# Lane marks by 32 narrow instructions, number products on GpSimd, and the inversion ahead of the turn sums

## The reference

```python
x  = L0_attn_u                                # (4, 512, 128)
xn = _layernorm(x)
# branch 1: a state-space layer, 4 heads of 64, state 128
z, xh, Bg, Cg, dd_dt, dd_A, trap, angles = split(xn @ W_in)
theta = cumsum(angles * dt)                   # over a sequence
K = rope(rmsnorm(Bg) * B_norm_w + B_bias, theta)
Q = rope(rmsnorm(Cg) * C_norm_w + C_bias, theta)
y = (chunked scan of decayed Q K^T products over xh) + D * xh
attn = (y * silu(z)) @ W_out
# branch 2: 16 experts, the best 2 of each token
probs = softmax(xn @ Wr + br); vals, idx = top_k(probs, 2)
for e in range(16):
    h = silu(xn @ W1[e]) * (xn @ W3[e])
    out += combine[:, e] * layernorm(h @ W2[e], gamma[e], beta[e])
return x + attn + out
```

## Time and profile before

| What | us |
|---|---|
| median of 3 runs | 285.36 (285.24 to 285.71) |
| the profiled execution | 283.92 |
| its span on the core | 282.2 |
| TensorE busy (matmul) | 252.1 |
| VectorE busy | 221.4 |
| GpSimd busy | 208.3 |
| ScalarE busy | 150.0 |

### The profile page before, as it was taken

One profiled execution on the slowest core, in us unless ns is written; L12 is line 12 of the kernel. 1 busy time (PEld: TensorE's weight loads), 2 busy tenths in 40 slices (PEclk: granted clock), 3 DMA queues, 4 the chain that ended last, 5 costly groups with the idle time before them and its releaser, 6 DMA issues.

```text
span 282.2 us, 7396 instructions
## 1 busy us (share of the span) xinstructions
PE 252.1 (89%) x2157; PEld 217.9 (77%) x2161; DVE 221.4 (78%) x604; ACT 150.0 (53%) x512; POOL 208.3 (74%) x284
## 2 busy tenths in 40 slices
PE   2999997799999999999999999999999999999600
PEld 0857964787897998899889979997998899889500
DVE  4778998778787969796979688787969796978446
ACT  1766996593456453755364645456453745363033
POOL 8656997698887787888887878887787875665400
PEclk9999999799999999999999999999999999999965
DMA  5630888665779778977889687988878987870096
GB/s 155 224 94 7 273 261 286 173 187 164 208 228 281 253 224 250 275 234 221 250 288 237 232 249 202 303 245 270 262 225 242 274 245 231 255 220 30 21 264 182
DMA packets 68856, 61.55 MB, mean 218 GB/s; under 512 B 6609, under 2 KB 52305, under 8 KB 68817
## 3 DMA queue, kind: packets, MB, share of 16 engines
q1 hardware_dynamic: 66256, 55.83, 65.5%
q0 software_dynamic: 2560, 5.25, 6.5%
HBM read 56.27 MB, written 4.78 MB: 216 GB/s over the span
## 4 chain that ended last, share of the span: by engine, by line
PE 60%; DVE 17%; ACT 6%; issue 6%; DMA 4%; POOL 4%; SPq 1%; DVEq 1%; POOLq 0%; ACTq 0%
PE bank L874 16%; PE bank L917 6%; PE bank L817 5%; PE bank L809 4%; PE bank L869 4%; PE bank L801 3%; PE bank L763 2%; PE bank L851 2%; PE bank L768 2%; DMA decay<-res_dram 2%; PE bank L913 2%; DVE rot L1360 2%; DVE sd L1376 2%; PE bank L833 2%; PE bank L860 1%
## 5 line engine op out<-in xcount | busy, mean ns | idle before, releaser
L874 PE MATMUL bank<-blkT,w_up 128*128 128x128 f32 x512 | 64.7, 280 | 1.5 <-DVE xrow L1410 0.6
L874 PEld LDWEIGHTS bank<-blkT,w_up 128*128 128x128 f32 x512 | 61.4, 195 | 4.2 <-issue 2.3
L633 POOL DMA_INDIRECT res_dram<-xrow,sidx x40 | 40.7, 1017 | 21.9 <-DVE xrow L1438 17.7
L580 POOL DMA_INDIRECT blk<-xn_dram,gidx x40 | 42.7, 1067 | 8.5 <-issue 7.3
L917 PE MATMUL bank<-w,xrow 128*128 128x128 f32 x256 | 34.6, 278 | 0.3 <-DVE xrow L1425 0.3
L1113 ACT ACTIVATE xrow<-bank 128x512 f32<-128x512 f32 x40 | 25.2, 629 | 15.2 <-PE bank L874 11.2
L917 PEld LDWEIGHTS bank<-w,xrow 128*128 128x128 f32 x256 | 31.1, 192 | 1.6 <-issue 1.6
L1410 DVE TENSOR_TENSOR xrow<-xrow,bank 128x512 f32<-128x512 f32 x40 | 27.3, 682 | 4.4 <-issue 4.2
L1342 DVE SCALAR_TENSOR_TENSOR kq<-sd,rms,bias_kq 128x512 f32<-128x512 f32 x32 | 23.2, 765 | 8.5 <-POOL rms L591 7.5
L626 POOL TENSOR_TENSOR rstd<-mv,mhalf 128x1 f32<-128x1 f32 x40 | 25.2, 629 | 0.3
L1107 ACT ACTIVATE blkT<-bank 128x128 f32<-128x128 f32 x40 | 12.2, 306 | 24.5 <-PE bank L860 20.9
(11 more groups left out here) (250 smaller groups left out, 617.1 us busy)
## 6 DMA issues: line engine op xcount, KB each, us to landing
w_up<-in_L_ffn_W_dram SPq DMA_DIRECT2D x96, 256.0 KB
w<-in_L_ffn_W_dram SPq DMA_DIRECT2D x48, 256.0 KB
e_row<-e_dram SPq DMA_DIRECT2D x16, 256.0 KB
decay<-l_dram SPq DMA_DIRECT2D x4, 512.0 KB, 6.0
gam<-in_L_ffn_gamma_dram SPq DMA_DIRECT2D x32, 64.0 KB
shift_y<-in_L_ffn_beta_dram SPq DMA_DIRECT2D x32, 64.0 KB
acc<-in_L_attn_u_dram SPq DMA_DIRECT2D x4, 256.0 KB, 3.7
xn_dram<-xrow SPq DMA_DIRECT2D x4, 256.0 KB, 5.1
```

The lines of the kernel that those rows point to most:

```text
L580: g.indirect_dma_start(out=blk[:, b % SLOTS, :], out_offset=None, in_=xn_dram, in_offset=bass.IndirectOffsetOnAxis(ap=gidx[:, entry(b):ent ...
L633: g.indirect_dma_start(out=res_dram, in_=res[:, b % HALF, :], in_offset=None, out_offset=bass.IndirectOffsetOnAxis(ap=sidx[:, entry(b):ent ...
L874: last = m(bank[out][:, c * P:(c + 1) * P], w_up[:, u % SETS, n, c * P:(c + 1) * P], blkT[:, b % 2, :], start=True, stop=True)
```

## The change

- Lane marks: two instructions of 2048 columns (`tensor_tensor`, both operands broadcast) become 32 of 128 columns (`tensor_scalar`, the token's lane number as a column operand in fp32).
- Block marks: the two compares stand one behind the other ahead of the lane marks; the products with the numbers become `mark(k)` on GpSimd, between the cuts.
- The expert of each block is worked out on GpSimd, ahead of the angle products; `pick_experts` goes from VectorE.
- The products and reductions that give the slots are done for both choices at once.
- TensorE does `invert(0)` and `invert(1)` in front of `sum_turns(1)` to `sum_turns(3)`; three dummy matmuls (`WARM_BLOCKS`) go.
- On VectorE `cut_turns(0)` and `mean_square(0)` come ahead of the row indices; `cut_turns(2)` and `cut_turns(3)` move back in `begin()`; in tile 1 `norm_kq` comes behind `product`.
- On GpSimd two of the eight cuts come behind the first gather, the first norm's power ahead of the second gather, and `weigh_q(0)` into tile 1.
- On ScalarE the logarithm of the gains comes ahead of the compares, the first squares two tiles earlier, the table load and the first sines earlier in `begin()`; tile 1 has another order.
- Some semaphores are merged, some scratch tiles share or change places.

```diff
-        bn_kq = sd[:, 0:2, :]
+        bn_kq = sd[:, 2:4, :]
...
+            pool.wait_ge(counted, 1)
+            g.tensor_scalar(behind[0:NU], full_n[0:NU], NE - 0.5, -2.0 * NE, ALU.is_gt, ALU.mult)
+            link(g.tensor_tensor(full_n[0:NU], full_n[0:NU], mix_n[0:NU], ALU.add))
+            link(g.tensor_tensor(full_n[0:NU], full_n[0:NU], behind[0:NU], ALU.add))
+            g.tensor_scalar(full_n[0:NU], full_n[0:NU], 2.0 * NE, 2.0 * (NE - 1), ALU.add, ALU.min)\
+                .then_inc(expert_ready, 1)
...
-            for t in range(SUMMED, NT):
-                cut_rows(t)
+            def mark(k):
+
+                pool.wait_ge(spots_ready, k + 1)
+                rows = row_h[:, k * NT:(k + 1) * NT, :]
+                g.tensor_tensor(rows, rows, bc(val_h[:, k * NT:(k + 1) * NT], NB, 1), ALU.mult).then_inc(marks_ready, 1)
+            cut_rows(SUMMED)
+            mark(0)
+            cut_rows(SUMMED + 1)
+            mark(1)
+            cut_rows(SUMMED + 2)
+            cut_rows(SUMMED + 3)
+            cut_rows(NT - 4)
+            cut_rows(NT - 3)
             pool.wait_ge(xn_out, 16 * NBATCH)
             pool.wait_ge(gidx_ready, 1)
+            gather(0)
+            cut_rows(NT - 2)
+            cut_rows(NT - 1)
...
-            gather(0)
+            rms_pow(0)
             gather(1)
-            rms_pow(0)
...
                 if first and t > 0:
                     rms_pow(t)
+                if t == 1:
+                    weigh_q(0)
...
-                if first:
+                if first and t > 0:
                     weigh_q(t)
...
                 pe.wait_ge(hot_ready, k + 1)
+                pe.wait_ge(marks_ready, k + 1)
...
             invert(0)
+            invert(1)
             sum_turns(1)
             sum_turns(2)
-            invert(1)
             sum_turns(3)
...
-                for _ in range(WARM_BLOCKS):
-                    m(bank[6][:, :], ones_h[:, :], neg_h[:, :, :].rearrange("p h i -> p (h i)"), start=True, stop=True)
...
+            act.wait_ge(g_ready, 1)
+            a(lnG, gmax, ACT.Ln).then_inc(lng_ready, 1)
...
-            act.wait_ge(g_ready, 1)
-            a(lnG, gmax, ACT.Ln).then_inc(lng_ready, 1)
...
-                if t == SUMMED + 4:
+                if t == SUMMED + 2:
                     squares(0)
...
-                out_block(0)
                 nc.scalar.preload_act_table_set("silu_and_others")
                 act.wait_ge(rest_in, 16 * RESTS)
+                out_block(0)
+                sines(0)
                 silu(0)
                 out_block(1)
-                sines(0)
                 silu(1)
...
-                if first:
+                if t == 1:
+                    squares(t)
+                    sines(t)
+                    out_block(b0 + 1)
+                    silu(b0)
+                elif first:
                     sines(t)
                     squares(t)
+                if first:
                     weigh(t)
                     gates(t)
                     move_x(t)
...
-            pick_experts()
             dve.wait_ge(pos_used, 1)
-            tt(pick, oh1, posb, ALU.mult)
-            link(tt(sc1, oh2, posb, ALU.mult))
-            v.tensor_reduce(slot[:, 0, :], pick, X, ALU.add)
-            link(v.tensor_reduce(slot[:, 1, :], sc1, X, ALU.add))
+            link(tt(pick, chosen, bc(posb, TOPK, 0), ALU.mult))
+            link(v.tensor_reduce(slot, pick, X, ALU.add))
...
-            one_hots(0)
-            one_hots(1)
+            for k in range(TOPK):
+                tt(row_h[:, k * NT:(k + 1) * NT, :], bc(iota_k, NT, 0), bc(blk_h[:, k, :], NB, 1), ALU.is_equal)                    .then_inc(spots_ready, 1)
                 if k == 0:
                     dve.wait_ge(expert_psum, 1)
+                    ts(blk_e[:, :], bank[3][0:1, 0:NU], 0.5, None, ALU.mult).then_inc(blk_e_ready, 1)
+            for k in range(TOPK):
+                for t in range(NT):
+                    last = ts(lane_h[k][:, t, :], iota_l, s_lane[:, k, t:t + 1], None, ALU.is_equal)
+                last.then_inc(hot_ready, 1)
+            cut_turns(0)
+            mean_square(0)
...
-                mean_square(0)
-                for b in range(NBATCH - 1):
-                    cut_turns(b)
+                cut_turns(1)
                 dve.wait_ge(rest_in, 16 * RESTS)
 
-                dve.wait_ge(theta_psum, NBATCH)
+                dve.wait_ge(theta_psum, 1)
                 weigh_bc(0)
                 norm_kq(0)
+                cut_turns(2)
                 product(0)
-                cut_turns(NBATCH - 1)
                 rot_cosine(0)
                 rotate(0)
+                cut_turns(3)
                 product(1)
...
-                    norm_kq(t)
+                    if t > 1:
+                        norm_kq(t)
...
                     product(b0)
+                if t == 1:
+                    norm_kq(t)
```

More of the change, by code:

```diff
@@ L211, in build @@
         turns = scratch([P, NT, NH * NA])
-        lg, rt, sc1, posb, pick = (scratch([P, NT, NE]) for _ in range(5))
+        rt, posb = (scratch([P, NT, NE]) for _ in range(2))
+        pick = scratch([P, TOPK, NT, NE])
+        lg, sc1 = pick[:, 0], pick[:, 1]
         lnG = scratch([P, NT, NH])
@@ L232, in build @@
         e2 = scratch([P, NT])
-        oh1 = scratch([P, NT, NE])
-        oh2 = scratch([P, NT, NE])
+        chosen = scratch([P, TOPK, NT, NE])
+        oh1, oh2 = chosen[:, 0], chosen[:, 1]
         halves = scratch([P, NE])
@@ L1008, in _ @@
             act.wait_ge(act_step, 1)
-            a(sp_e, sp_x, ACT.Exp, scale=-1.0).then_inc(spe_ready, 1)
+            a(sp_e, sp_x, ACT.Exp, scale=-1.0).then_inc(spx_ready, 1)
             act.wait_ge(spu_ready, 1)
-            a(sp_l, sp_u, ACT.Ln).then_inc(spl_ready, 1)
-            act.wait_ge(spl_ready, 1)
-            a(sp_r, sp_l, ACT.Exp, scale=-1.0).then_inc(spr_ready, 1)
+            a(sp_l, sp_u, ACT.Ln).then_inc(spx_ready, 1)
+            act.wait_ge(spx_ready, 2)
+            a(sp_r, sp_l, ACT.Exp, scale=-1.0).then_inc(spx_ready, 1)
             for q in range(2 * NBATCH):
@@ L1148, in iteration @@
                     if b is not None:
-                        out_block(b + 1)
-                        silu(b)
+                        if t > 1 or b is not b0:
+                            out_block(b + 1)
+                            silu(b)
                         out_h(b - 1)
@@ L1240, in _, with cut_turns, mean_square @@
             link(tt(wtop[:, 1, :], wtop[:, 0, :], e2, ALU.mult))
-            def pick_experts():
-                dve.wait_ge(counted, 1)
-                ts(behind[0:NU], full_n[0:NU], NE - 0.5, -float(NE), ALU.is_gt, ALU.mult)
-                link(tt(full_n[0:NU], full_n[0:NU], mix_n[0:NU], ALU.add))
-                link(stt(full_n[0:NU], full_n[0:NU], 0.5, behind[0:NU], ALU.mult, ALU.add))
-                ts(full_n[0:NU], full_n[0:NU], float(NE), float(NE - 1), ALU.add, ALU.min).then_inc(expert_ready, 1)
+            def cut_turns(b):
+                sums = bank[THETA[b]]
+                dve.wait_ge(theta_psum, b + 1)
+                cut = turns[:, b * TB:(b + 1) * TB, :].rearrange("p j c -> p (j c)") if b >= 2 else cut_[b]
+                link(ts(cut, sums[:, :], MAGIC, -MAGIC, ALU.add, ALU.add))
+                tt(theta[:, b * TB:(b + 1) * TB, :].rearrange("p j c -> p (j c)"), sums[:, :], cut,
+                   ALU.subtract).then_inc(theta_ready, 1)
+            def mean_square(t):
+                dve.wait_ge(s["sq_done"], 2 * (t + 1))
+                again(dve, s["rms_ready"], t)
+                ts(ms[:, :], ms[:, :], 1.0 / DS, EPS, ALU.mult, ALU.add).then_inc(s["ms_ready"], 1)
             dve.wait_ge(tot_psum, 1)
@@ L1311, in _ @@
             tt(sidx[:, :], v_row, v_neg, ALU.add).then_inc(sidx_ready, 1)
-            def cut_turns(b):
-                sums = bank[THETA[b]]
-                dve.wait_ge(theta_psum, b + 1)
-                cut = turns[:, b * TB:(b + 1) * TB, :].rearrange("p j c -> p (j c)") if b >= 2 else cut_[b]
-                link(ts(cut, sums[:, :], MAGIC, -MAGIC, ALU.add, ALU.add))
-                tt(theta[:, b * TB:(b + 1) * TB, :].rearrange("p j c -> p (j c)"), sums[:, :], cut,
-                   ALU.subtract).then_inc(theta_ready, 1)
             def diagonal(t):
```

36 lines of the change are left out of this document (12 added, 24 removed).

## The result

The changed kernel is slower: 287.12 us median (286.42 to 287.52) against 285.24 us (284.96 to 285.71), a ratio of 1.006 with a 95% interval of 1.0041 to 1.008, which is 1.7 us. The loss is small, but clear of the noise. The forecast was 282.8 us. The profiled execution took 287.52 us with a span of 285.5 us, 0.4 us above its median, and the one of before (283.92 us) lay 1.3 us under the median of 285.24 us. That is why the two traces differ by 3.6 us and the medians by 1.9 us.

A forecast was written before the change was run, and what follows sets the result against it. It took TensorE, the busiest engine, as the bound, and asked when it reaches tile 1: 1.7 us earlier, plus 0.9 us inside tile 1, 2.6 us off the 285.36 us median, gives 282.8 us. The range was 280.2 to 288.9 us.

The forecast's parts named there:

- VectorE before the marks: VectorE ahead of the lane marks: expert steps leave (1.24 us), joined products and reductions save 0.65 us, compares end at 34.8 us.
- GpSimd at the gather: GpSimd ahead of the first gather: free at 42.3 us, nothing waits for it; the gather goes out at T + 2.95 us.
- the second product: GpSimd's second number product of 640 columns: 1.5 us taken for each, done near 39.6 us, ahead of T.
- T: End of the last lane mark on VectorE: 43.98 us before, forecast 41.5 us, 2.5 us earlier.
- The 0.8 us charged: VectorE between T and the gather: cut_turns(0) and the mean square ahead of the row indices cost 0.8 us.
- The sums and the clock: TensorE's inversion and three turn sums end at T + 7.2 us; 0.5 us charged for a slow clock stretch.
- The pause it named ahead of T: A new gap of TensorE from 39.6 to 41.5 us, which might bring a slow clock costing 1.8 us.
- the last of the three ways in which it said it could be wrong: A slow clock falls on TensorE's turn sums, and they outlast the gather.
- ScalarE as the next in line: Late cut, exponentials, 1.28 us table load and block's copy on ScalarE hold rise(0) until T + 8.95 us.
- the way to tile 1: From T to TensorE's start of tile 1: T + 15.85 us, with 0.5 us charged for the clock T + 16.35 us.
- Rises at full clock: TensorE's two rises, 2.88 and 2.47 us before, take 1.79 us at full clock, as sums fill the gap.
- Tile 1: Reordered work inside tile 1 takes 0.9 us of the 1.1 us that TensorE idled there for VectorE.

The follow-up runs named there:

- clock_dummies: The changed kernel with 14 dummy matmuls ahead of invert(0) and 10 between the two inversions: 286.3 us, ratio 1.0063 to the kernel before.
- before_dummies: The kernel before with 12 instead of 3 dummy matmuls in front of the first block's transpose: 283.62 us, ratio 0.9959.
- tile1_alone: The kernel before with only the order of tile 1's work changed: 284.6 us, ratio 0.9981 (0.9961 to 1.0001).
- wide_marks: The changed kernel with two lane marks of 2048 columns in place of 32, number products still on GpSimd: 285.02 us, ratio 1.0001.
- narrow_back: The changed kernel with number products back on VectorE and the 32 narrow lane marks kept: 286.8 us, ratio 1.0052 to the kernel before.
- marks_back: The changed kernel with number products and wide lane marks back on VectorE: 284.01 us, ratio 0.9962 to the kernel before.
- two_sums_first: The changed kernel with sum_turns(1) and sum_turns(2) put back ahead of both inversions: 287.88 us, ratio 1.0111 to the kernel before.
- front_steps: The kernel before with only VectorE's relief ahead of the slots (expert steps on GpSimd, joined products and reductions, earlier logarithm): 285.86 us, ratio 1.0019.

## Why the prediction was wrong

**VectorE before the marks.** Relief as forecast: compares end at 34.7 us (34.8 forecast), product and reduction 0.99 and 0.69 us (0.95 and 0.7).

**GpSimd at the gather.** Right: nothing waits for the second product (done at 38.8 us), the gather 2.84 us after T (2.95 forecast). The 0.8 us charged for cut_turns(0) and the mean square ahead of the indices was off the path in the changed kernel, though: the sums outlasted the gather.

**The sums and the clock.** The second wrong term. The prediction had the sums end at T + 7.2 us and charged 0.5 us for a slow stretch; they ended at T + 9.9 us. The pause it named ahead of T (39.6 to 41.5 us, 1.9 us) was there, but in two pieces of 3.58 and 1.89 us, since the marks were late, and the slow stretch (41 to 51 us) lay right on the sums. That is the last of the three ways in which it said it could be wrong. The trace of clock_dummies puts the stretch at 2.8 us on the sums and 1.6 us at tile 1, though its time shows no gain. ScalarE as the next in line, the table load behind the late exponentials, came out as worked out: it is what kept 1.2 us of that from counting. rise(0) began at T + 10.66 us and not at T + 8.95 us, and the two rises and what follows took 0.3 us longer than reckoned. Less the 0.5 us charged, these are the 1.5 us by which the way to tile 1 was reckoned too short.

**Rises at full clock.** Right, but the size of the gain was not: the 1.79 us were a piece of the chain of waits, which is counted only from the end of the piece before it, while the 2.88 and 2.47 us are whole durations. At full clock a rise lasts 2.02 to 2.05 us in that view, in the changed kernel and in before_dummies. The slow clock in the kernel before cost the rises 0.86 and 0.42 us, 1.3 us and not 1.8, and 0.85 us of it reached tile 1 in before_dummies.

**Tile 1.** 0.9 us was taken; tile1_alone shows 0.92 us in tile 1 and 0.44 us after tile 2. The step left out the tile behind. In the changed kernel the two gave 0.52 us.

Put together: T 3.45 us later than forecast, the way 1.54 us longer and 0.38 us less from tile 1 are 5.4 us, and 282.8 us would become 288.1 us. The median is 287.12 us. Part of the missing 1.0 us is the trace of before, on which the differences were built. Its first gather landed 3.9 us after its issue. In tile1_alone, with the same work up to there, it took 4.3 us, the first rise took 3.19 us, and tile 1 began 0.8 us later (with the start of the gather taken off). How the rest divides was not settled.

## What to carry to other kernels

Before a wide instruction on VectorE is cut into many narrow ones, count what GpSimd has queued beside it: in these runs each of its instructions cost one narrow one its whole length, and only what was left ran at its own speed; a wide one paid once, and made GpSimd pay. A row that shows an instruction running freely proves little if hardly anything ran on the other engine, or if its type and operands were others. And when a producer of TensorE is made later or its filler moved behind, price the pause before it and the slow stretch after it as one term, on whatever work comes next: it moved with the order here, and matmuls of no use filled it. Then look at the time as well as the trace: of the three kernels with such matmuls only the kernel before got faster by its ratio.

## What the runs showed of the hardware

- Turns between VectorE and GpSimd are not shared evenly. Beside narrow marks a GpSimd cut took 0.63 us, the same as alone; beside a wide mark it took 2.67 us (wide_marks). Marks that come every 0.162 us by themselves came once in 0.60 us beside cuts and once in 1.2 us beside number products, as the times of the groups have it.
- VectorE's compares and products of 640 columns take 0.81 and 0.82 us with GpSimd idle (narrow_back, from 40.34 us) and 1.25 and 1.14 us beside its cuts (marks_back).
- The first gather, the same transfer each time, landed 3.4 to 4.8 us after its issue in the profiles where TensorE waited for it (two_sums_first and front_steps at the ends). That is as much as some of the terms argued over here, and a reason not to build on one trace for them.
